# A recommendation tower on one TensorE: the second field comes by four gathers of whole rows and is turned by TensorE, and the first products run in another order

## The chip, the cores and the metric

One core of one Trainium2 chip runs the whole program. The metric is the device time of the program in microseconds (us), from start to end. Below, TensorE (PE in the profile), VectorE (DVE), ScalarE (ACT), GpSimd (POOL) and SyncE (SP) are the core's engines; GpSimd issues the gathers and the adding transfers here, SyncE the plain loads of weights.

## The reference

512 rows, 8 embedding tables of width 1024 (H). All is float32.

```
e = stack([tbl_f[ids[:, f]] for f in range(8)])          # 512 x 8 x 1024
t  = tanh(relu(e[:, not_idx] @ Wn1 + bn1) @ Wn2 + bn2)    # the two "not" fields; iv = e with these replaced
def pair_fuse(pairs, W1, b1, W2, b2):
    v = concat([iv[:, pairs[:, 0]], iv[:, pairs[:, 1]]])  # width 2048
    return relu(v @ W1 + b1) @ W2 + b2
z = (sum of 2 and-pairs + 1 or-pair + fields in no pair) / count
h = relu([z, dense_ctx] @ W_top1 + b_top1); h = relu(h @ W_top2 + b_top2); y = h @ W_top3
```

Which fields are "not" fields and which form pairs is an input (not_idx, and_pairs, or_pairs), so the rows to fetch are worked out on the chip.

## The kernel before, in words

**Layout.** Activations are held with the hidden index on the 128 partitions: XR has 8 buffers of 8 k-tiles x 512 batch columns. A float32 product is made of three fast ones: each operand is split into a rounded high part (ScalarE, an fp32r copy) and a low part (VectorE, the difference), and TensorE adds high x high, high x low and low x high. XO holds the split activations (8 k-tiles, so the operands of two entries), WO the split weights (two pieces), WR seven raw pieces of 512 KB as they come from memory.

**The work list.** The time line is a list of entries (a matrix product of a 512-wide quadrant, over 4 k-tiles) and each entry has 4 quarters t, one per PSUM bank of output. A quarter is 4 k x 3 = 12 matmuls of 128x512. The first 28 entries are three stages, in which two matrices of the batch's fields (Wn1 and then Wn2 for stages 0 and 1, Wa1 in two halves for stage 2) are multiplied by seven products instead of eight: P1, P2, Q5, Q6, Q7, P4, Q3. For it VectorE makes the sums S1, S3, S2, S4 of the activations' quadrants (operand_sum), and sums of weight quadrants are made by GpSimd's adding transfers (add_quadrant). Piece n serves quarters 2n and 2n+1. The quadrants of the activations of stage 0 are the halves of the two "not" fields: a11, a12 of the first and a21, a22 of the second, so P1 and P2 need only the first field, and S1 = a21 - a22 needs the second.

**What sets the order.** Each engine has a program written out by hand; at quarter t ScalarE and VectorE do, in this order, the split of weight piece t//2+1, the split of the next entry's operand, evacuations of PSUM (kept: ScalarE's copy; combine: VectorE's addition, then ScalarE's activation), the turning of gathered fields (TURNS_AT) and the sums (SUMS_AT). They are all in-order queues, tied by counting semaphores.

**Fields.** The first "not" field comes by four gathers of 128 whole rows (x0_in), is transposed by TensorE with the identity as weights (turn_x0), split by ScalarE and VectorE out of PSUM, and copied to XR (x0_raw). Every other field comes by 16 gathers of quarter rows (gather_half, 2 x 8; line 427) and is turned by four 32x32-block transposes of VectorE over 128x1024 (line 782). The first field that is so brought is slot 1, the second "not" field; slots 2 to 7 are the pairs. Ahead of them, VectorE computes the row numbers (slot_rows) and some constants; setup_done comes at the end of these.

**Start.** keep_running issues small products of the identity with itself, 28 of them while the first rows are on their way, so that TensorE isn't idle. The first product starts when all four tiles of the first field are turned (k-tiles 0 to 3). The third entry (Q5, the first that needs S1) runs in two halves of 256 columns each (BY_HALVES), so that its first half can start when half the batch of the second field is there.

Lines of the profile that matter: L950 all large products, L978 turns of the first field, L983 keep_running, L710 low part of weights, L521 high part, L765/L768/L771 low part of activations, L755 low part out of PSUM, L832 operand_sum, L846 combine, L915 the sum of weights for the first Q5, L782 the 32x32 turn, L421/L427 gathers, L440 adding transfers.

## Time and profile before

| | us |
|---|---|
| median of 3 runs | 548.82 (546.6 to 549.87) |
| the profiled execution, whole | 549.19 |
| its span, from the first to the last instruction | 547.1 |
| TensorE busy | 529.2 (97%) |
| VectorE busy | 360.5 (66%) |
| ScalarE busy | 242.4 (44%) |
| GpSimd busy | 242.5 (44%) |

The profiled execution is 0.4 us above the median, and 2.1 us of it lie around the span. Busy shares are averages over the span; what a stretch waits for is read from that stretch alone. A matmul's listed duration (about 390 ns) overlaps the next one's; the pace is read from a long row's time over its count.

### The profile page before, as it was taken

How to read it: one execution, taken by the hardware profiler on the slowest of the kernel's cores; microseconds unless marked ns; L12 is line 12 of the kernel's file. 1: busy time of each engine (PE TensorE's matmuls, PEld its weight loads, DVE VectorE, ACT ScalarE, POOL GpSimd, SP SyncE). 2: the span in 40 equal slices, each digit the busy share in tenths (PEclk: the TensorE clock that was granted, in tenths of full speed). 3: DMA queues.
4: the chain of work that ended last, by engine and by line, in shares of the span. 5: the costliest groups of instructions: out<-in, count | busy, mean ns of one | idle time of the engine just before them, and what ended most of it. 6: DMA issues, size and time to landing. Idle time of an engine off the chain costs nothing.

```text
span 547.1 us, 6141 instructions
## 1 busy us (share of the span) xinstructions
PE 529.2 (97%) x2392; PEld 438.8 (80%) x2392; DVE 360.5 (66%) x371; ACT 242.4 (44%) x291; POOL 242.5 (44%) x182
## 2 busy tenths in 40 slices
PE   6988999997999999999999999999999999999998
PEld 6868788885878888888888888888888888888885
DVE  7498886988757885888556678752332874245832
ACT  2733666626457544443536444323243423142343
POOL 5765877884888344130087017754445300000000
PEclk9999999998999999999999999999999999999999
DMA  7858965347786565367199425999999982331000
GB/s 260 298 168 162 196 205 177 108 127 119 156 205 195 118 115 177 78 100 131 38 195 314 127 98 167 276 246 247 248 247 246 246 264 80 115 93 40 1 0 1
DMA packets 38703, 87.31 MB, mean 160 GB/s; under 512 B 4401, under 2 KB 4657, under 8 KB 38674
## 3 DMA queue, kind: packets, MB, share of 16 engines
q0 software_dynamic: 18720, 49.29, 41.8%
q1 hardware_dynamic: 19522, 37.51, 21.5%
q8 instruction: 19, 0.31, 0.2%
q10 hardware_dynamic: 432, 0.11, 0.1%
q14 instruction: 10, 0.08, 0.0%
HBM read 86.90 MB, written 0.00 MB: 159 GB/s over the span
## 4 chain that ended last, share of the span: by engine, by line
PE 70%; POOL 14%; DVE 6%; DMA 4%; issue 4%; ACT 1%; DVEq 0%; ACTq 0%
PE PS L950 68%; POOL XR L427 12%; DMA WR<-weights 3%; DVE WO L710 2%; DVE XR L782 1%; DMA XR<-table,rows 1%; POOL XR L421 1%; POOL WR L440 1%; PE PS L1099 1%; DVE XR L832 1%; PE PS L1071 1%; DVE XR L846 1%; ACT WO L521 0%; DVE XO L765 0%; DMA XR<-ints 0%
## 5 line engine op out<-in xcount | busy, mean ns | idle before, releaser
L950 PE MATMUL PS<-XO,WO 128*128 128x512 f32 (+1 forms) x2256 | 506.3, 386 | 10.6 <-DVE WO L710 8.8
L950 PEld LDWEIGHTS PS<-XO,WO 128*128 128x128 f32 x2256 | 417.4, 188 | 97.5 <-DVE WO L710 10.9
L521 ACT ACTIVATE WO<-WR 128x1024 fp32r<-128x1024 f32 x93 | 98.6, 1060 | 254.6 <-PE PS L950 232.9
L710 DVE TENSOR_TENSOR WO<-WR,WO 128x1024 fp32r<-128x1024 f32 x93 | 113.7, 1224 | 144.4 <-ACT WO L521 144.2
L427 POOL DMA_INDIRECT XR<-table,rows x112 | 147.7, 1319 | 58.5 <-issue 33.5
L556 ACT ACTIVATE XO<-XR 128x1024 fp32r<-128x1024 f32 (+1 forms) x74 | 77.3, 1045 | 2.2 <-PE PS L950 1.9
L440 POOL DMA_DIRECT2D WR<-weights x30 | 37.2, 1627 | 85.7 <-DVE WO L710 59.6
L771 DVE TENSOR_TENSOR XO<-XR,XO 128x1024 fp32r<-128x1024 f32 x58 | 70.4, 1215 | 0.7 <-ACT XO L556 0.7
L498 POOL DMA_INDIRECT XR<-table,rows_rest x32 | 52.4, 1638 | 40.3 <-DMA XR<-table,rows_rest 38.5
L782 DVE STREAM_TRANSPOSE XR<-XR 128x1024 f32<-128x1024 f32 x28 | 59.7, 2137 | 4.3 <-DMA XR<-table,rows 4.3
L832 DVE TENSOR_TENSOR XR<-XR 128x1024 f32<-128x1024 f32 (+1 forms) x32 | 38.5, 1222 | 0.1
L561 ACT ACTIVATE XR<-XR,col 128x512 f32<-128x512 f32 x36 | 25.6, 715 | 11.0 <-DVE XR L846 11.0
L846 DVE TENSOR_TENSOR XR<-PS,XR 128x512 f32<-128x512 f32 x36 | 24.4, 679 | 3.5 <-PE PS L950 2.6
L587 ACT ACTIVATE XR<-PS 128x512 f32<-128x512 f32 x36 | 21.3, 594 | 6.2 <-PE PS L950 6.2
L768 DVE SCALAR_TENSOR_TENSOR XO<-XR,XO 128x1024 fp32r<-128x1024 f32 x16 | 19.5, 1218 | 0.3 <-ACT XO L556 0.2
L983 PE MATMUL PS<-ident 128*128 128x128 f32 x40 | 8.8, 392 | 5.0 <-DVE ident L700 5.0
L983 PEld LDWEIGHTS PS<-ident 128*128 128x128 f32 x40 | 8.2, 304 | 5.0 <-DVE ident L700 5.0
L860 DVE SCALAR_TENSOR_TENSOR XR<-PS,inv,XR 128x512 f32<-128x512 f32 x8 | 6.0, 750 | 6.5 <-PE PS L950 6.3
L592 ACT ACTIVATE XR<-PS,col 128x512 f32<-128x512 f32 x12 | 8.1, 677 | 0.7 <-PE PS L950 0.7
L755 DVE TENSOR_TENSOR XO<-PS,XO 128x512 fp32r<-128x512 f32 x8 | 5.0, 682 | 3.7 <-ACT XO L616 3.7
L616 ACT ACTIVATE XO<-PS 128x512 fp32r<-128x512 f32 x8 | 4.1, 603 | 7.2 <-PE PS L978 7.2
L865 DVE TENSOR_TENSOR XO<-XR,XO 128x512 fp32r<-128x512 f32 x4 | 2.8, 692 | 6.6 <-ACT XO L609 6.5
(68 smaller groups left out, 98.5 us busy)
## 6 DMA issues: line engine op xcount, KB each, us to landing
WR<-weights SPq DMA_DIRECT2D x71, 512.0 KB, 4.8
WR<-weights POOLq DMA_DIRECT2D x30, 512.0 KB, 8.1
XR<-table,rows POOLq DMA_INDIRECT x116, 3.9
XR<-table,rows_rest POOLq DMA_INDIRECT x32, 12.7
XR<-dense_t SPq DMA_DIRECT2D x3, 32.0 KB, 3.4
XR<-w_dense SPq DMA_DIRECT2D x3, 32.0 KB, 3.0
XR<-ints SPq DMA_DIRECT2D x1, 84.0 KB, 2.1
XR<-identity ACTq DMA_DIRECT2D x1, 64.0 KB, 3.6
```

The costliest lines, as they stand in the source:

```text
L427: pool.indirect_dma_start(to[:, QC * g:QC * (g + 1)], None, table_quarters, bass.IndirectOffsetOnAxis(ap=rows[:, slot - 1, 8 * h + g:8 * h ...
L440: pool.dma_start(raw_piece(slot), quadrant_rows(8 * matrix_of(e) + 4 * mh + 2 * h, kh), accum_op=ALU.add).then_inc(w_sum[slot], 16)
L498: pool.indirect_dma_start(rest_tile(b), None, table, bass.IndirectOffsetOnAxis(ap=rows_rest[:, b, f:f + 1], axis=0), compute_op=ALU.add if ...
L521: nc.scalar.activation(WO[:, n % 2, 0, :], WR[:, slot, :], ACT.Copy).then_inc(w_hi, 1)
L556: nc.scalar.activation(XO[:, s1:s1 + 2, 0, :], source(e, kk, regs), ACT.Copy, scale=scale)\
L561: nc.scalar.activation(place(s, which, m), place(s, which, m), FUNC[s], bias=bias_of(s, which, m)).then_inc(c_out[which], 1)
L710: V_.tensor_tensor(WO[:, n % 2, 1, :], WR[:, raw_slot(n), :], WO[:, n % 2, 0, :].bitcast(FP32), ALU.subtract).then_inc(w_lo, 1)
L771: V_.tensor_tensor(lo, source(e, kk, regs), hi, ALU.subtract).then_inc(x_lo, 1)
L782: V_.transpose(XR[:, SLOT_BUF[slot], :, b:b + 128].rearrange("p k (g b) -> p g k b", b=32), staging(slot, h)[:, 1024 * (i % 2):1024 * (i % ...
L832: V_.tensor_tensor(out, one, two, ALU.subtract).then_inc(sums, 1)
L846: V_.tensor_tensor(place(s, to, m), PS[:, BANK_B + m, :], place(s, to, m), op).then_inc(dve_ev, 1)
L950: mm = nc.tensor.matmul(PS[:, bank, cols], WO_t[:, slot, ws, i, k, :], XO[:, x0 + k, xs, cols], start=first and k == 0 and n == 0, stop=la ...
```

## The change

In words, in the order of the program:

- Row numbers of both "not" fields are computed together; the second field comes by four gathers of whole rows right behind the first's (x1_in), not by 16 of quarter rows. GpSimd then waits for setup_done before it gathers slots 2 and on.
- The first field is turned and split in two halves of the batch, in pairs of k-tiles: TensorE turns tiles 0 and 1 of the batch ahead of the first product, and tiles 2 and 3 between the products. Entry 0 (P1) is the one that runs in halves of 256 columns, and not Q5 any more.
- The second field is turned by 32 transposes of TensorE, 16 of them between the last products of entry 0 and 16 behind it; VectorE copies it from PSUM to XR by 8 copies (x1_keep). Its four 32x32 turns are gone.
- VectorE computes the pair slots' rows and the constants behind the low parts of the first half of the batch, and ahead of those of the second half.
- keep_running: 18 in place of 28, and 2+2+2 in place of 2+2+2+6.
- The products of stages 0 and 1 run in the order P1, P2, Q5, Q3, Q6, Q7, P4 (before: P1, P2, Q5, Q6, Q7, P4, Q3). Sums, loads, adding transfers, turns and evacuations move with it; P2 and Q5 (stage 0) and Q5 (stage 1) are now kept by ScalarE. Stages swap their halves of k and some buffers, so that each can start with what the one before has ready first.
- Stage 2 and what follows keep their order of products.

The diff, cut to its core:

```diff
-IDLE_PRODUCTS = 28
+ORDER = [(P1, P2, Q5, Q3, Q6, Q7, P4), (P1, P2, Q5, Q3, Q6, Q7, P4), (P1, P2, Q5, Q6, Q7, P4, Q3)]
+IDLE_PRODUCTS = 18
-BY_HALVES = 2
+KEPT = [{P1: "C11", P2: "C21", Q5: "C22", Q6: "C12"}, {P1: "C11", Q5: "C22", Q6: "C12"},
+        {P1: "C11", Q6: "C12", Q7: "C22"}]
+COMBINED = [{P2: ("C11", 9, 10), Q6: ("C12", 2, 3), Q7: ("C22", 1, 2)},
+            {P2: ("C11", 2, 3), Q6: ("C12", 2, 3), Q7: ("C22", 1, 2)}, ...
 SUMS_AT = {
-    (0, S1, 0): (2, 8), (0, S3, 0): (2, 9), (0, S2, 0): (9, 9), (0, S4, 0): (12, 13),
+    (0, S1, 0): (2, 3), (0, S3, 0): (4, 5), (0, S2, 0): (5, 6), (0, S4, 0): (7, 8),
-TURNS_AT = {1: (1, 1, 7, 7), 2: (15, 16, 19, 23), 3: (24, 27, 28, 32), 4: (36, 40, 44, 47),
+TURNS_AT = {2: (6, 8, 10, 12), 3: (14, 17, 19, 21), 4: (24, 27, 35, 38),
...
@@ SyncE
-            load(8)
+            load(6)
+            for n, split in ((7, 2), (10, 3), (11, 6), (16, 7)):
+                load_after(n, split)
@@ GpSimd
+            for b in range(BT):
+                pool.indirect_dma_start(flat(ROW1_BUF)[:, H * b:H * (b + 1)], None, table,
+                                        bass.IndirectOffsetOnAxis(ap=rows0[:, 1, b:b + 1], axis=0))\
+                    .then_inc(x1_in[b], 16)
-            pool.wait_ge(rows1_ready, 1)
+            pool.wait_ge(setup_done, 1)
             for h in range(2):
-                gather_half(1, h)
-            pool.wait_ge(setup_done, 1)
-            gather_half(2, 0, range(4))
-            for j in (Q6, Q7):
-                for h in range(2):
-                    add_piece(0, j, h)
-            gather_half(2, 0, range(4, 8))
+                gather_half(2, h)
+            gather_half(3, 0)
+            add_piece(0, Q7, 0)
+            for h in range(2):
+                add_piece(0, Q6, h)
+            add_piece(0, Q7, 1)
+            gather_half(3, 1)
...
@@ ScalarE
+            def x0_hi(h, pair):
+                act.wait_ge(x0_turned, x0_done(h, pair))
+                nc.scalar.activation(XO[:, 2 * pair:2 * pair + 2, 0, half_batch(h)], x0_bank(pair), ACT.Copy)\
+                    .then_inc(x_hi, 1)
+            def x0_keep(h, pair):
+                act.wait_ge(x_lo, x0_done(h, pair))
+                nc.scalar.activation(XR[:, 0, 2 * pair:2 * pair + 2, half_batch(h)], x0_bank(pair), ACT.Copy)\
+                    .then_inc(x0_raw, 1)
...
@@ VectorE
-            slot_rows(1, 1).then_inc(rows1_ready, 1)
-            slot_rows(2, 6)
             split_w(0)
             split_w(1)
+            for pair in range(4):
+                x0_lo(0, pair)
+            slot_rows(2, 6)
...
+            for pair in range(4):
+                x0_lo(1, pair)
+            def x1_keep(h):
+                for pair in range(4):
+                    dve.wait_ge(x1_turned, x0_done(h, pair))
+                    V_.tensor_copy(XR[:, 1, 2 * pair:2 * pair + 2, half_batch(h)], x0_bank(pair)).then_inc(x1_raw, 1)
+            x1_keep(0)
...
+                    if t == 2:
+                        x1_keep(1)
@@ TensorE
-            for b in range(BT):
+            for b in range(2):
                 pe.wait_ge(x0_in[b], 16)
                 for k in range(4):
...
+            def turn_second_field(h, first):
+                for k in range(first, first + 4):
+                    if k % 2 == 0:
+                        pe.wait_ge(*((x1_raw, x0_done(0, k // 2)) if h else (x0_raw, x0_done(1, k // 2))))
+                    for b in range(2 * h, 2 * h + 2):
+                        pe.wait_ge(x1_in[b], 16)
+                        turn = turn_rows(ROW1_BUF, b, k)
+                    if k % 2:
+                        turn.then_inc(x1_turned, 1)
...
+                            mm = product(bank0 + m, m // 2, m % 2, x0, i == 0, True,
+                                         x0_there if m == 0 else None, half_batch(i))
+                            if (i, m) == (0, 1):
+                                turn_second_half(0)
+                            elif (i, m) == (1, 0):
+                                turn_second_half(4)
+                            elif (i, m) == (1, 1):
+                                turn_second_field(0, 0)
+                            elif (i, m) == (1, 2):
+                                turn_second_field(0, 4)
+                    for k in (0, 4):
+                        turn_second_field(1, k)
```

The order of VectorE's instructions at its start. Each row is a line, an operation, out<-in by the program's names (XO split activations, WO split weights, PS PSUM) and a shape, with xN for N in a row. Before, the row numbers of the pair slots (L690, L694, L696) stand ahead of the first two weight splits:

```order
L706 TENSOR_SCALAR XR<-XR 128x8
L690 TENSOR_TENSOR XR<-XR 128x128 x6
L694 TENSOR_REDUCE XR<-XR 128x96
L696 CAST rows<-XR 128x96
L710 TENSOR_TENSOR WO<-WR,WO 128x1024 x2
L717 TENSOR_REDUCE XR<-XR 128x1
```

In the changed kernel the same place reads:

```order
L767 TENSOR_SCALAR XR<-XR 128x8
L771 TENSOR_TENSOR WO<-WR,WO 128x1024 x2
L777 TENSOR_TENSOR XO<-PS,XO 128x2x256 x4
L752 TENSOR_TENSOR XR<-XR 128x128 x6
L756 TENSOR_REDUCE XR<-XR 128x96
L758 CAST rows<-XR 128x96
L786 TENSOR_REDUCE XR<-XR 128x1
```

The row numbers, and all the constants behind them down to setup_done, now stand behind the low parts (L777) of the first half of the first field.

VectorE again, from the instruction that sets setup_done (L751, now L820) to the split of weight piece 4, the last rows here. Before:

```order
L751 TENSOR_SCALAR final_bias<-final_bias,inv 128x8
L755 TENSOR_TENSOR XO<-PS,XO 128x512 x8
L782 STREAM_TRANSPOSE XR<-XR 128x4x8x32 x2
L710 TENSOR_TENSOR WO<-WR,WO 128x1024
L832 TENSOR_TENSOR XR<-XR 128x4x256 x2
L915 TENSOR_TENSOR WR<-WR 128x1024 x2
L710 TENSOR_TENSOR WO<-WR,WO 128x1024
L846 TENSOR_TENSOR XR<-PS,XR 128x512 x2
L710 TENSOR_TENSOR WO<-WR,WO 128x1024
```

In the changed kernel (L830 is the copy of the second field, L906 operand_sum, L998 the sum of weights, L844 the low part of activations):

```order
L820 TENSOR_SCALAR final_bias<-final_bias,inv 128x8
L777 TENSOR_TENSOR XO<-PS,XO 128x2x256 x4
L830 COPY XR<-PS 128x2x256 x4
L771 TENSOR_TENSOR WO<-WR,WO 128x1024
L830 COPY XR<-PS 128x2x256 x4
L906 TENSOR_TENSOR XR<-XR 128x4x256
L998 TENSOR_TENSOR WR<-WR 128x1024 x2
L906 TENSOR_TENSOR XR<-XR 128x4x256
L771 TENSOR_TENSOR WO<-WR,WO 128x1024
L906 TENSOR_TENSOR XR<-XR 128x4x256
L844 TENSOR_TENSOR XO<-XR,XO 128x2x512
L906 TENSOR_TENSOR XR<-XR 128x4x256 x2
```

Piece 3's split (the second L771) is now behind eight copies, and behind it come four operations before piece 4's (L771, the next row, not shown), three of them sums.

GpSimd's queue from its first gathers on. Before (L427 are gathers of quarter rows, L440 adding transfers):

```order
L421 DMA XR<-table,rows 128x1024 x4
L427 DMA XR<-table,rows 128x256 x20
L440 DMA WR<-weights 128x2x512 x4
L427 DMA XR<-table,rows 128x256 x4
L440 DMA WR<-weights 128x2x512 x2
L427 DMA XR<-table,rows 128x256 x32
L440 DMA WR<-weights 128x2x512 x6
```

In the changed kernel (L480 and L494 are the same two kinds):

```order
L469 DMA XR<-table,rows 128x1024 x4
L473 DMA XR<-table,rows 128x1024 x4
L480 DMA XR<-table,rows 128x256 x24
L494 DMA WR<-weights 128x2x512 x4
L480 DMA XR<-table,rows 128x256 x8
L494 DMA WR<-weights 128x2x512 x2
L480 DMA XR<-table,rows 128x256 x8
L494 DMA WR<-weights 128x2x512 x2
```

The first adding transfers stand behind 24 gathers of quarter rows (20 before), and the run of 32 gathers ahead of stage 1's first additions is cut up into three runs of 8.

## Rows read from the trace of the kernel before

**Rows 1.** Busy time by stretch: stretch, its us, then each engine, TensorE's clock, DMA share, GB/s
```profile
16.00:60.00 44.00, 39.03 (x219) 33.43 (x220) 35.81 (x34) 22.22 (x33) 28.66 (x25) 1.00 0.78 215
...
165.00:537.00 372.00, 372.00 (x1658) 308.36 (x1657) 229.03 (x215) 156.18 (x177) 123.84 (x89) 1.00 0.62 154
```
**Rows 2.** Timeline of TensorE: start, us, what, xcount [idle before it <- who released it]
```profile
5.04 6.23 PE L983 MATMUL PS<-ident 128*128 128x128 f32 x28 [5.04 <-DVE ident L700]
...
16.14 2.99 PE L950 MATMUL PS<-XO,WO 128*128 128x512 f32 x12 [0.55 <-DVE XO L755]
18.97 1.93 PE L978 MATMUL PS<-ident,XR 128*128 128x128 f32 x16
20.66 8.44 PE L950 MATMUL PS<-XO,WO 128*128 128x512 f32 x36
31.32 5.76 PE L950 MATMUL PS<-XO,WO 128*128 128x512 f32 x24 [2.22 <-DVE WO L710]
37.22 8.65 PE L950 MATMUL PS<-XO,WO 128*128 128x512 f32 x48 [0.15 <-DVE WO L710]
47.08 3.13 PE L950 MATMUL PS<-XO,WO 128*128 128x256 f32 x24 [1.21 <-DVE WO L710]
50.63 6.01 PE L950 MATMUL PS<-XO,WO 128*128 128x256 f32 x48 [0.42 <-DVE XO L765]
57.47 65.59 PE L950 MATMUL PS<-XO,WO 128*128 128x512 f32 x288 [0.82 <-DVE XO L768]
127.02 34.27 PE L950 MATMUL PS<-XO,WO 128*128 128x512 f32 x144 [3.96 <-DVE WO L710]
162.52 326.86 PE L950 MATMUL PS<-XO,WO 128*128 128x512 f32 x1440 [1.23 <-DVE WO L710]
```
**Rows 3.** Busy time by stretch around the stall at 123 us (columns as in the first group)
```profile
127.00:130.00 3.00, 2.98 (x7) 2.40 (x8) 3.00 (x4) 2.04 (x4) 1.19 (x1) 0.51 0.28 20
```
**Rows 4.** Chain of waits, ahead of the stall at 123 us: start, us, what
```profile
107.33 9.56 POOL XR L427
117.19 0.94 POOL XR L427
118.13 6.50 DMA WR<-weights
```
**Rows 5.** The second gather's row in GpSimd's timeline, and line 421's landing
```profile
5.61 1.03 POOL L421 DMA_INDIRECT XR<-table,rows  x1 [0.30 <-issue]
...
DMA to landing us min/median/max: 4.6/5.3/5.4
```
**Rows 6.** Timeline of ScalarE and VectorE at the start and around 111 us
```profile
14.67 2.07 ACT L616 ACTIVATE XO<-PS 128x512 fp32r<-128x512 f32 x4 [6.31 <-PE PS L978]
15.30 2.48 DVE L755 TENSOR_TENSOR XO<-PS,XO 128x512 fp32r<-128x512 f32 x4 [1.27 <-ACT XO L616]
26.06 4.10 DVE L782 STREAM_TRANSPOSE XR<-XR 128x1024 f32<-128x1024 f32 x2 [3.33 <-DMA XR<-table,rows]
111.41 3.52 DVE L832 TENSOR_TENSOR XR<-XR 128x1024 f32<-128x1024 f32 x3
114.82 1.25 DVE L710 TENSOR_TENSOR WO<-WR,WO 128x1024 fp32r<-128x1024 f32 x1
```
**Rows 7.** Costliest groups, line 427: xcount | busy, mean ns | idle before, releaser
```profile
L427 POOL DMA_INDIRECT XR<-table,rows x112 | 147.7, 1319 | 58.5 <-issue 33.5
```
**Rows 8.** Line 440, adding transfers: ns min/median/max, then landing
```profile
L440 POOL DMA_DIRECT2D WR<-weights x30: 1179/1361/3180, 39.8 to 275.9; - x30
DMA to landing us min/median/max: 5.9/8.1/19.8
```
**Rows 9.** Timeline of VectorE's setup: its first and last rows
```profile
5.52 1.30 DVE L690 TENSOR_TENSOR XR<-XR 128x128 f32<-128x128 f32 x6
7.97 2.35 DVE L710 TENSOR_TENSOR WO<-WR,WO 128x1024 fp32r<-128x1024 f32 x2
13.81 0.23 DVE L751 TENSOR_SCALAR final_bias<-final_bias,inv 128x8 f32<-128x8 f32 x1
```

More of the change, by code:

```diff
@@ L128 @@
 R_SLOT = 4
-R_PIECES = [2 * e + h for s in range(3) for j in (P2, Q7, Q3) for half in range(STAGE_HALVES[s])
+R_PIECES = [2 * e + h for s in range(3) for j in ORDER[s] if j in (P2, Q7, Q3) for half in range(STAGE_HALVES[s])
             for e in [entry_of(s, j, half)] for h in range(2)]
@@ L271, in dlrm_tower @@
         quarter = sem("quarter")
[L272 removed]
+        field_in = {(s, h): sem(f"field_in{s}_{h}") for s in range(2, SLOTS) for h in range(2)}
         turned = sem("turned")
@@ L775, in turn @@
                 dve.wait_ge(field_in[slot, h], 16 * 8)
-                if i == 0 and slot > 1:
+                if i == 0 and slot == 2:
+                    dve.wait_ge(x1_turned, x0_done(1, 3))
+                if i == 0 and slot > 2:
                     dve.wait_ge(turned, turned_count(slot - 1, 1))
```

336 lines of the change are left out of this document (185 added, 151 removed), and 2 rows, old and new, of the table slot.

## The prediction

> **What bounds the kernel now.** I read the busy time by stretch first, then TensorE's timeline, then what each of its waits leads back to. From 165 us on TensorE is busy all of the time, while VectorE is busy for 229 of 372 us [rows 1]: nothing that the change moves there can bring time, as long as it hides. From 16 to 60 us TensorE is busy for 39.0 of 44 us and VectorE for 35.8. The timeline says where the rest is [rows 2]: the first product starts at 16.14; then TensorE idles 2.22, 0.15, 1.21, 0.42 and 0.82 us before it reaches quarter 12 at 57.47 (together 4.82), 3.96 before quarter 36 at 127.02, and 1.23 before quarter 48 at 162.52. That is 10.0 us of idleness behind the first product. The stall of 3.96 costs more than itself: behind it the granted clock stands at 0.50, the 1.2 GHz level, for three microseconds [rows 3]; the 144 matmuls from 127.02 took 34.27 us where the 1440 of the last row go at 0.227 us each, 32.7 for 144 [rows 2], so 1.5 us went with the clock. Its cause is GpSimd's queue: one gather held it for 9.56 us, and the adding transfer behind it landed 6.5 us after 118.13 [rows 4].
>
> **Prices.** From [rows 2]: a quarter of 12 full matmuls 2.72 us; one of 12 half-wide ones 6.01 / 4 = 1.50; a turn on TensorE (20.66 - 18.97) / 16 = 0.106, eight of them 0.85. From [rows 6]: a VectorE operation over 1024 columns starts (114.82 - 111.41) / 3 = 1.14 us behind the one before; a 32x32 turn 2.05; one over 512 columns out of PSUM 2.48 / 4 = 0.62; a ScalarE copy 2.07 / 4 = 0.52 over 512 columns, and so about 1.04 over 1024. The copy of the second field out of PSUM has no row; between half of 0.62 and a 1024-wide operation's 1.14 I take 0.62, since it reads as many columns from PSUM. The Trainium skill, VectorE: DVE Perf Modes, section The perf-mode tier table, holds an fp32 operation with a PSUM operand to one element a cycle for copies too, which speaks for 0.62 against its half; no row here shows such a copy.
>
> **The first product.** The second tile's gather starts at 5.61 and lands 5.3 us later [rows 5], and one more small multiplication stands before them (0.2): the second tile is there at about 11.1. Eighteen warm-up products at 6.23 / 28 = 0.22 us end at 9.0 [rows 2]. Then TensorE has 4 turns, 2 warm-ups, 8 turns and 2 warm-ups to do. At this time of before a small product still takes 0.22 us, a turn near 0.2: 3.1 us, so 14.2. The data are earlier: turned pair at 11.5, ScalarE at 11.7, VectorE 0.63 behind it [rows 6], product 0.84 behind that (16.14 - 15.30), 13.2. So TensorE itself decides: **14.2, 1.9 us earlier**.
>
> **Entry 0.** Four half quarters and 8 turns: to 21.1. The second half's low parts stand on VectorE behind the setup. VectorE has the first half's low parts done at about 16.1 (ScalarE must also copy two pairs to XR between them). The row numbers took 7.97 - 5.52 = 2.45 and the constants 14.04 - 10.32 = 3.7 us [rows 9]: setup_done at 22.3 (before 14.0), first low part of the second half lets the product run at 23.2. **Stall 2.1 us**. What is queued behind this: GpSimd, whose gathers of slot 2 wait for setup_done. Then 4 half quarters (6.0), 40 turns (4.2): entry 1 starts at 33.4. Their operands (copies of ScalarE, whole rows issued from 10.3 to 14.1 at the place of the first quarter-row gathers) are there some 3 us ahead, by a landing of 5.3; even the longest landing of an adding transfer, 19.8 [rows 8], behind 10.3 would cost only 3 us.
>
> **VectorE sets quarters 6 to 12.** It copies the second field's first half until 31.2 (the turns end at 30.3), then does piece 2's split, 4 copies, S1, two weight sums, S1, piece 3's split: 1.14 + 4 x 0.62 + 5 x 1.14 = 9.3, at 40.5. TensorE would be at quarter 6 at 33.4 + 5.45 = 38.9: **stall 1.7**. Then S3, x, S3, S2, piece 4: 5.7, at 46.2, TensorE ready at 46.0: **0.2**. Then x, a 32x32 turn, S2, S4, piece 5: 6.6, at 52.8, TensorE at 51.7: **1.1**. Then a turn and S4 (3.2), and here ScalarE is in the way: it can make the high part of Q3's operand only from S4, in front of piece 6's high part; 1.04 + 0.5 (a kept bank) + 1.04 + 1.14, so 59.9 or 60.0, TensorE ready at 58.3: **1.7**. Quarter 12 starts at 60.0; it was 57.47. So the start, whose field arrives by a shorter way, gives nothing back: **+2.5 us**. It is made of -1.9 (start), +3.4 (32 turns more) and 6.8 us of stalls for 4.8, which makes 3.5; the other -1.0 is what the rows of before run over my prices behind each wait (24 matmuls in 5.76 us for 5.45), and which isn't paid where VectorE sets the time.
>
> From quarter 12 to 24 VectorE has 12 splits, 6 turns and 10 combinations: 13.7 + 12.3 + 10 x 0.6 = 32.0 us, at 92.0, while TensorE comes to quarter 24 at 92.7. It hides by less than a microsecond, against the 2.7 us that each quarter lasts; if a combination costs 0.7, TensorE waits 0.3.
>
> **The two stalls of before.** Quarter 36 comes at 60.0 + 65.6 = 125.6 without a wait, if Q5's summed pieces of stage 1 are there. Their additions now stand behind runs of 8 gathers and not behind 32 in a row, and are issued as soon as VectorE has split P1's pieces, at about 102 and 107 us; they are needed at about 120, so that even a hold of 9.56 us would leave them in time. The 3.96 and its 1.5 of clock go. So does the 1.23 in front of P4: its additions stood behind eight gathers (the x8 and x2 of GpSimd's rows), and now follow the other additions at once, some seven quarters ahead of their use. From quarter 48 on the two kernels have the same work. Sum: +2.5 - 3.96 - 1.5 - 1.23 = **-4.2 us**. Against the profiled execution's 549.2 that is 545.0; the median of runs is 0.4 lower, so **544.6 us**. ScalarE's 4 kept banks more (2.1 us) hide under its 56% idle time.
>
> **Rivals.** (A) VectorE keeps up: the stalls of 1.7, 0.2, 1.1 and 1.7 vanish, because TensorE turns later or the copies cost half. 544.6 - 4.8 = **539.8**. For it: VectorE was idle for 8 of the 44 us of this stretch [rows 1], and 8.2 us of turns go for 5 of copies. Against it: its queue is in order, and the sums for the new order of products all come in quarters 2 to 8. (B) The first additions come late by a little: GpSimd issues 24 gathers behind 22.3, then adds. Piece 8's addition is issued at 22.3 + 24p + 1.5 and lands 8.1 later [rows 8]; ScalarE needs it at 70.9 (quarter 16) - 2.4 = 68.5. p was 1.32 + 0.3 of issue (33.5 / 112) on the mean, 1.62 with the long ones [rows 7], and 0.94 + 0.3 in a short one [rows 4], the bound from below: landing between 62.0 and 70.9. At 1.62 TensorE waits 2.4, **547.0**, which can't be told from no change. (C) The slower side: a hold of 9.56 us as in [rows 4] falls into these 24 gathers. From p = 1.4 (65.6) it adds 8.3: 5.4 us late, and as that is more than the 3.96 that brought the clock down, 1.5 on top: **551.5**. From such a delay on it is slower beyond what a measurement misses; at a p of 1.25 the same hold would end within it. Nothing in the rows says where such a hold falls; one of this length in 112 gathers [rows 4, 7] gives 24 of them a chance of about 0.2, and half of it hits where the margin is thin. (D) The clock falls in the stretch with the turns: at half rate the 96 half-wide matmuls cost 96 x 0.1 more and the 64 turns 6: up to 15 us, **559**. Against it: behind 16 turns in a row and behind a stall of 2.22 us the rows go at full pace [rows 2]. The Trainium skill, TensorE: Matmul & The Clock Gate, section Part 4: PE-mode transpose, says that transposes don't count as busy for the clock; by that rule this kernel, with runs of turns between short products, would be the place for (D), and it is the rule that speaks against the change.
>
> **The numbers.** Forecast as walked, between 542.5 (half of VectorE's stalls not there) and 546.5: 0.50. (A) 0.17. (B) 0.16. (C) 0.12. (D) 0.05. The range holds what lies between half-way past (A) and (B) with the lesser part of (C): 539.5 to 549.5, with 0.15 to 0.2 left out; the likeliest case's own is 542.5 to 546.5. A measurement of this kernel tells about 0.5% from no change, 2.7 us. Faster than 546.1: nearly all of the forecast's 0.50 and (A), 0.64. Same: (B) and a rest, 0.20. Slower than 551.5: half of (C) and more, (D): 0.16.
>
> **What would show it.** Right: first large product near 14.2; idle of about 2 us in front of entry 0's second half, released by VectorE's L777; waits of 1 to 2 us released by L771 at quarters 6, 10 and 12; quarter 12 near 60; no idle near 125 and 160, and a clock of 1.00 throughout. Wrong: a wait of ScalarE for an adding transfer near 68 us (B, C), a clock of 0.50 between 14 and 34 us (D), or quarter 12 before 57.5 (A).

## The result, and the profile after

The changed kernel is slower: 551.09 us (549.46 to 553.0, 20 runs) against 547.89 (540.82 to 551.5, 20 runs) for the kernel before, a ratio of 1.0089 [1.0066, 1.0112]. Ratios are taken over the runs within 1.5% of the fastest of their kernel, here 13 of the 20 of the kernel before; the means of all 20 give 1.0066. The profiled execution took 550.46, its span 548.7.

TensorE's timeline of the changed kernel, which answers to [rows 2]:
```profile
14.72 3.31 PE L1031 MATMUL PS<-XO,WO 128*128 128x256 f32 x24
...
23.29 1.70 PE L1031 MATMUL PS<-XO,WO 128*128 128x256 f32 x12 [1.48 <-DVE XO L777]
...
31.83 1.96 PE L1060 MATMUL PS<-ident,XR 128*128 128x128 f32 x16
33.55 5.71 PE L1031 MATMUL PS<-XO,WO 128*128 128x512 f32 x24
40.70 11.43 PE L1031 MATMUL PS<-XO,WO 128*128 128x512 f32 x48 [1.44 <-DVE WO L771]
53.01 5.76 PE L1031 MATMUL PS<-XO,WO 128*128 128x512 f32 x24 [0.88 <-DVE WO L771]
60.10 11.21 PE L1031 MATMUL PS<-XO,WO 128*128 128x512 f32 x48 [1.34 <-DVE WO L771]
75.50 415.39 PE L1031 MATMUL PS<-XO,WO 128*128 128x512 f32 x1824 [4.19 <-DVE WO L771]
```
Up to quarter 12 it runs as walked: there at 60.10. The stalls of 3.96 and 1.23 us of [rows 2] are gone, and 1824 matmuls follow one another from quarter 16 on. But in front of quarter 16 stands a stall of 4.19 us that the kernel before doesn't have. The chain of waits names it (start, us, what):
```profile
22.91 0.95 POOL XR L480
...
61.18 0.94 POOL XR L480
62.12 0.79 POOL WR L494
62.91 10.20 DMA WR<-weights
73.14 1.06 ACT WO L575
74.23 1.24 DVE WO L771
75.50 4.54 PE PS L1031 x12
```
The lines left out are 22 more gathers and the 0.30 us of issue ahead of each. GpSimd issues 24 gathers in a row, (62.12 - 22.91) / 24 = 1.63 us each, then the first adding transfer, which lands 10.2 us later; ScalarE and VectorE pass its piece on, and TensorE, free since 71.31, had nothing to multiply. The granted clock was 1.00 before the stall and 0.50, the 1.2 GHz level, behind it. Busy time by stretch (PE, PEld, DVE, ACT, POOL, granted clock, DMA share, GB/s):
```profile
16.00:60.00 44.00, 38.96 (x233) 33.55 (x232) 38.41 (x69) 19.26 (x29) 30.38 (x23) 1.00 0.52 172
77.00:80.00 3.00, 3.00 (x9) 2.33 (x8) 3.00 (x4) 1.88 (x3) 2.69 (x3) 0.50 1.10 261
```
At the pace of [rows 2], 0.227 us, the 1824 matmuls take 414.0; they took 415.4, so the clock cost 1.4 us. The new stall costs 5.6 us with its clock. The two old ones cost 3.96 + 1.23 + 1.5 = 6.7, so the tail gains 1.1; quarter 12 comes 60.10 - 57.47 = 2.6 later. Together that is the 1.6 by which the spans differ (548.7 against 547.1).

What stretches the gathers stands in the timelines of GpSimd and VectorE side by side:
```profile
33.70 0.95 POOL L480 DMA_INDIRECT XR<-table,rows  x1 [0.30 <-issue]
34.95 1.97 POOL L480 DMA_INDIRECT XR<-table,rows  x1 [0.30 <-issue]
...
46.31 1.97 POOL L480 DMA_INDIRECT XR<-table,rows  x1 [0.30 <-issue]
48.59 0.95 POOL L480 DMA_INDIRECT XR<-table,rows  x1 [0.30 <-issue]
...
32.49 2.48 DVE L830 COPY XR<-PS 128x512 f32<-128x512 f32 x4
34.89 1.21 DVE L906 TENSOR_TENSOR XR<-XR 128x1024 f32<-128x1024 f32 x1
...
46.24 1.22 DVE L844 TENSOR_TENSOR XO<-XR,XO 128x1024 fp32r<-128x1024 f32 x1
47.38 2.20 DVE L857 STREAM_TRANSPOSE XR<-XR 128x1024 f32<-128x1024 f32 x1
```
While VectorE copies from PSUM or turns 32x32 blocks a gather takes 0.95 us, as at 33.70 and 48.59. From 34.89 to 47.38 VectorE does operations with two operands in SBUF one behind the other, and all six gathers of that time take 1.96 or 1.97: each ends 0.9 us behind the next start of an operation (the gather of 34.95 at 36.92, the operation's start at 36.02). In all, the 24 gathers take 39.2 - 24 x 1.25 = 9.2 us more than short ones would.

The 9.56 us of [rows 4] look like the long form of it. VectorE's timeline of the kernel before:
```profile
106.91 1.21 DVE L771 TENSOR_TENSOR XO<-XR,XO 128x1024 fp32r<-128x1024 f32 x1
108.02 1.24 DVE L832 TENSOR_TENSOR XR<-XR 128x1024 f32<-128x1024 f32 x1
...
115.96 2.17 DVE L782 STREAM_TRANSPOSE XR<-XR 128x1024 f32<-128x1024 f32 x1
```
Between these stand six more operations with two SBUF operands, the last at 114.82 [rows 6]. The gather starts at 107.33, inside the first of the eight, is held over the seven boundaries between them, and ends at 116.89, 0.93 behind the start of the 32x32 turn. The Trainium skill, SBUF — State Buffer, section SBUF: two separate sides, describes the port pair that VectorE and GpSimd share as an exclusive lock, held for the whole instruction; a VectorE operation with two SBUF inputs takes it only against a GpSimd operation that reads SBUF, and where the page has GpSimd unable to write descriptors it speaks of another kind, an operation of VectorE in a 2-port mode. The traces agree with a lock by a two-input operation, as far as a gather, whose row numbers lie in SBUF, is held to the end of one (1.97); a hold over seven boundaries between operations the page doesn't have.

### The profile page after: what moved, and what is told of

The parts are those of the page before. It is cut to its first block, busy times and chain, and to the rows that moved or that the text cites. A ratio compares the mean times of both kernels' runs of the same rounds, so it can differ in the third digit from the quotient of the medians.

```text
span 548.7 us, 6197 instructions
## 1 busy us (share of the span) xinstructions
PE 531.1 (97%) x2408; PEld 440.8 (80%) x2408; DVE 357.4 (65%) x373; ACT 244.4 (45%) x295; POOL 218.3 (40%) x170
## 4 chain that ended last, share of the span: by engine, by line
PE 86%; POOL 6%; DMA 3%; DVE 2%; issue 2%; ACT 1%
PE PS L1031 84%; POOL XR L480 6%; DMA WR<-weights 2%; DMA XR<-table,rows 1%; PE PS L1211 1%; PE PS L1183 1%; DMA XR<-ints 0%; DVE XO L777 0%; PE PS L1218 0%; DVE WO L771 0%; DVE XR L752 0%; ACT XR L665 0%; POOL XR L469 0%; ACT XO L659 0%; ACT WO L575 0%
## 5 line engine op out<-in xcount | busy, mean ns | idle before, releaser
L771 DVE TENSOR_TENSOR WO<-WR,WO 128x1024 fp32r<-128x1024 f32 x93 | 113.9, 1225 | 148.3 <-ACT WO L575 148.0
L480 POOL DMA_INDIRECT XR<-table,rows x96 | 119.7, 1246 | 67.5 <-issue 28.0
L604 ACT ACTIVATE XO<-XR 128x1024 fp32r<-128x1024 f32 (+1 forms) x76 | 79.4, 1046 | 16.1 <-DVE XR L906 14.2
L494 POOL DMA_DIRECT2D WR<-weights x30 | 37.2, 1598 | 101.8 <-DVE WO L771 68.8
L844 DVE TENSOR_TENSOR XO<-XR,XO 128x1024 fp32r<-128x1024 f32 x60 | 73.2, 1221 | 2.7 <-ACT XO L604 2.7
L857 DVE STREAM_TRANSPOSE XR<-XR 128x1024 f32<-128x1024 f32 x24 | 51.6, 2151 | 0.0
L906 DVE TENSOR_TENSOR XR<-XR 128x1024 f32<-128x1024 f32 (+1 forms) x32 | 38.4, 1217 | 0.0
L929 DVE TENSOR_TENSOR XR<-XR,PS 128x512 f32<-128x512 f32 x16 | 11.1, 691 | 2.2 <-PE PS L1031 2.1
L1060 PE MATMUL PS<-ident,XR 128*128 128x128 f32 x64 | 10.4, 314 | 1.3 <-DMA XR<-table,rows 1.3
L929 DVE TENSOR_TENSOR XR<-PS,XR 128x512 f32<-128x512 f32 x16 | 10.8, 679 | 1.3 <-PE PS L1031 1.3
L1065 PE MATMUL PS<-ident 128*128 128x128 f32 x24 | 6.1, 423 | 4.6 <-DVE ident L761 4.6
L1060 PEld LDWEIGHTS PS<-ident,XR 128*128 128x128 f32 x64 | 8.8, 199 | 1.7 <-DMA XR<-table,rows 1.7
L777 DVE TENSOR_TENSOR XO<-PS,XO 128x512 fp32r<-128x512 f32 x8 | 5.1, 685 | 6.3 <-ACT XO L659 6.3
L1065 PEld LDWEIGHTS PS<-ident 128*128 128x128 f32 x24 | 5.6, 332 | 4.6 <-DVE ident L761 4.6
```

Source lines behind the costliest of these rows:

```text
L480: pool.indirect_dma_start(to[:, QC * g:QC * (g + 1)], None, table_quarters, bass.IndirectOffsetOnAxis(ap=rows[:, slot - 2, 8 * h + g:8 * h ...
L494: pool.dma_start(raw_piece(slot), quadrant_rows(8 * matrix_of(e) + 4 * mh + 2 * h, kh), accum_op=ALU.add).then_inc(w_sum[slot], 16)
L604: nc.scalar.activation(XO[:, s1:s1 + 2, 0, :], source(e, kk, regs), ACT.Copy, scale=scale)\
L771: V_.tensor_tensor(WO[:, n % 2, 1, :], WR[:, raw_slot(n), :], WO[:, n % 2, 0, :].bitcast(FP32), ALU.subtract).then_inc(w_lo, 1)
L844: V_.tensor_tensor(lo, source(e, kk, regs), hi, ALU.subtract).then_inc(x_lo, 1)
L857: V_.transpose(XR[:, SLOT_BUF[slot], :, b:b + 128].rearrange("p k (g b) -> p g k b", b=32), staging(slot, h)[:, 1024 * (i % 2):1024 * (i % ...
```

## The experiments

Each ratio is against the kernel before on the same chip, beside the kernel named. The kernel before takes about 548 us on some chips and 565 on others; every kernel profiled on the latter, w1 nearly excepted, shows gaps of TensorE before quarter 12 which no instruction releases, so totals of the two kinds of chip aren't compared. The tail, from quarter 12's first product to the end of the span, can be: it is 489.6 before and 488.6 after. "c1 = a1" means the same kernel again. The profiled executions (the stalls of 2.94 in a1, 0.75 in w1, 2.17 in w2, 2.22 in g1 and 0.58 in i2 lie behind 290 us and are gaps that nothing releases, not waits for GpSimd; they are in the tail's time):

| kernel | quarter 12 at | tail | longest stall in the tail | median (before beside it) | ratio |
|---|---|---|---|---|---|
| a1 additions first | 76.02 | 491.5 | 2.94, 2.70 | 569.07 (565.96) | 1.0089 [1.0037, 1.0141] |
| b later gathers apart | 73.36 | 484.9 | 1.36 | 566.14 (565.96) | 1.0014 [0.9968, 1.0059] |
| c0 the changed kernel | 59.27 | 489.8 | 4.58 | 550.86 (547.64) | 1.0089 [1.0049, 1.0129] |
| c1 = a1 | 59.47 | 489.5 | 2.97 | 550.81 | 1.0068 [1.0031, 1.0105] |
| c2 setup earlier | 58.05 | 488.9 | 2.85 | 550.14 | 1.0064 [1.0018, 1.011] |
| c3 both | 60.94 | 488.2 | 2.94 | 551.20 | 1.0089 [1.0039, 1.0139] |
| w1 changed, few gathers | 62.15 | 483.6 | 0.75 | 547.32 (565.18) | 0.9653 [0.959, 0.9716] |
| w2 before, few gathers | 68.98 | 484.9 | 2.17 | 554.92 | 0.9812 [0.9724, 0.99] |
| d1 a1 + late turns | 74.94 | 484.3 | 0.47 | 561.42 | 0.995 [0.9919, 0.998] |
| g1 changed + memsets | 86.21 | 485.0 | 2.22 | 572.38 | 1.0108 [1.0031, 1.0186] |
| i1 before + memsets | 73.44 | 483.0 | none | 559.75 (564.52) | 0.997 [0.992, 1.0019] |
| i2 = g1 | 84.32 | 483.3 | 0.58 | 571.83 | 1.0171 [1.011, 1.0231] |
| i3 = d1 | 74.68 | 484.3 | 0.56 | 561.10 | 0.9977 [0.9941, 1.0013] |
| i4 = d1 + memsets | 75.26 | 483.0 | none | 560.39 | 0.9967 [0.9932, 1.0002] |
| j1 = i4 | 59.44 | 483.9 | 0.62 | 545.87 (548.35) | 0.9964 [0.9936, 0.9991] |
| j2 = i1 | 57.55 | 482.5 | none | 541.83 | 0.9888 [0.9847, 0.9929] |

**The additions ahead of slot 3's gathers (a1, c1).** The theory at first: the first additions are late behind 24 gathers, and nothing else is wrong.
```
+            add_piece(0, Q7, 0)
+            for h in range(2):
+                add_piece(0, Q6, h)
             gather_half(3, 0)
-            add_piece(0, Q7, 0)
-            for h in range(2):
-                add_piece(0, Q6, h)
             add_piece(0, Q7, 1)
```


> The changed kernel, with GpSimd's three adding transfers for Q7 and Q6 moved ahead of slot 3's first eight gathers; nothing else. Theory (late additions): the changed kernel loses 4.19 us of idleness in front of quarter 16 and about 1.4 us of clock behind it because those transfers are issued only at 62.1 us, behind 24 gathers that took 39.2 us. Then this kernel issues the first two near 49 us and the third near 53, the stall at 71.3 us and the 0.50 clock behind it are gone, quarter 12 stays at 60.1, and the time falls by 5.6 us, from 551.1 to about 545.5. Rival (the additions are slow by themselves, by contention with the loads and each other, 10.2 us to landing): they still land late, the stall shrinks by less than half, and the time stays above 549.

> Again the changed kernel with three adding transfers ahead of slot 3's first eight gathers. Theory (late additions): no stall in front of quarter 16, and 5.6 us below the changed kernel of the same chip. Rival (contention makes them late wherever they stand): less than 2.5 us below it.

c1's TensorE timeline behind quarter 12:
```profile
59.47 16.63 PE L1031 MATMUL PS<-XO,WO 128*128 128x512 f32 x72 [1.32 <-DVE WO L771]
76.49 27.89 PE L1031 MATMUL PS<-XO,WO 128*128 128x512 f32 x120 [0.39 <-DVE WO L771]
107.35 383.86 PE L1031 MATMUL PS<-XO,WO 128*128 128x512 f32 x1680 [2.97 <-DVE WO L771]
```
The stall at quarter 16 is gone, 0.39 stands at quarter 18 (76.49) and 2.97 at quarter 28 (107.35), with 1680 matmuls that take 2.5 us over pace behind it. The theory expected 5.6 us less and got 0.05 (550.81 against c0's 550.86): it fell. VectorE's timeline shows the new place:
```profile
95.39 1.21 DVE L771 TENSOR_TENSOR WO<-WR,WO 128x1024 fp32r<-128x1024 f32 x1
100.92 2.19 DVE L857 STREAM_TRANSPOSE XR<-XR 128x1024 f32<-128x1024 f32 x1 [4.32 <-DMA XR<-table,rows]
104.94 1.23 DVE L844 TENSOR_TENSOR XO<-XR,XO 128x1024 fp32r<-128x1024 f32 x1 [1.83 <-issue]
```
VectorE waits 4.32 us for slot 4's gathers at its turn in quarter 24, then idles another 1.83 for nothing that the profile names, and the split that TensorE needs is queued behind. What GpSimd puts first it takes from what it puts last.

**Setup in VectorE's early gap, and both (a2, c2, a3, c3).** slot_rows moves ahead of split_w(0), the first half's low parts behind the constants, so that GpSimd starts earlier. c0 is the changed kernel unedited beside them.
```
+            slot_rows(2, 6)
             split_w(0)
             split_w(1)
-            for pair in range(4):
-                x0_lo(0, pair)
-            slot_rows(2, 6)
...
+            for pair in range(4):
+                x0_lo(0, pair)
             for pair in range(4):
                 x0_lo(1, pair)
```


> The changed kernel, with VectorE's row numbers ahead of its first two weight splits and the constants right behind these, in front of the first half's low parts; GpSimd's queue is untouched. VectorE idled 2.3 us ahead of the first split and 2.9 us behind the second in the changed kernel, and the moved work is 6.1 us. Theory: setup_done comes near 14 and not at 22.6 us, the stall of 1.48 us in front of entry 0's second half goes, gathers of quarter rows start near 15 and not at 22.9, so the additions are issued near 54 and the 4.19 us in front of quarter 16 go too, with their clock: about 544. The first product may move by up to 1 us (14.7 to 15.5). Rival (the early DMA traffic is the limit: gathers that start 8 us earlier collide with the weight loads and only stretch): additions issued after 58 us and a time above 548.

> Both moves together. Theory: no stall in front of quarter 16 and none in front of entry 0's second half; the additions have a margin of ten microseconds or more. As VectorE alone then sets quarters 6 to 12, the time is that of the setup move within 0.5 us, about 544. Rival (they add up beyond it): below 542.

> The changed kernel itself, unedited, beside the next two on one chip. The runs so far of the kernels with a moved piece were on a chip where the kernel before takes 566 us and TensorE idles between single instructions with nothing that the profile names (gaps of 0.3 to 2.4 us between 20 and 45 us). Expectation: if this chip is like the first one, 551 us, a stall of about 4.2 us in front of quarter 16 and a clock of 0.50 behind it; if such gaps appear again, 1.009 times before or more.

> Again the changed kernel with VectorE's setup in its idle gaps. Theory (setup_done comes too late): the stall ahead of entry 0's second half and that ahead of quarter 16 gone, 7 us below the changed kernel of the same chip. Rival, formed on the other chip: gathers that start at 15 us keep the DMA engines full from 18 to 40 us, and TensorE's gaps between single instructions come with it, so that entry 0 takes 10 to 30 us longer and the kernel is slower than the changed one. A gain says the gaps belong to that chip, a loss that they belong to the traffic.

> Again both moves. Theory: as the setup move within 0.5 us. Rival (gaps from traffic): slower than the kernel with the additions moved alone, by what its gaps between 18 and 45 us show.

a2 and a3 took 1.0199 [1.0125, 1.0272] and 1.011 [1.0068, 1.0153]; a2's profiled execution, at 589.05 far above its median of 576.43, isn't read. The theory of a gain of 7 us fell on both kinds of chip. c2 has the stall of entry 0 gone and quarter 12 at 58.05, 1.2 ahead of c0, and loses it again: 1.99 at 87.53 and 2.85 at 135.20. GpSimd's timeline, then VectorE's, shows where the last comes from:
```profile
110.97 7.06 POOL L480 DMA_INDIRECT XR<-table,rows  x1 [0.30 <-issue]
118.33 1.02 POOL L480 DMA_INDIRECT XR<-table,rows  x1 [0.30 <-issue]
...
114.73 2.35 DVE L906 TENSOR_TENSOR XR<-XR 128x1024 f32<-128x1024 f32 x2
117.22 1.23 DVE L771 TENSOR_TENSOR WO<-WR,WO 128x1024 fp32r<-128x1024 f32 x1
```
The one gather lasts from 110.97 to 118.03; VectorE's only gap in that time, 114.73 + 2.35 = 117.08 to 117.22, stands 0.95 ahead of its end. Four orders of the same work on one chip, four tails of 488 to 490: where the stall falls depends on the order; that there is one holds in all four.

**The kernel before, with Q5's additions of stage 1 ahead of slot 4's gathers (b).**
```
+            for h in range(2):
+                add_piece(1, Q5, h)
             gather_half(4, 0)
-            for j in (Q5, Q6, Q7):
+            for j in (Q6, Q7):
                 for h in range(2):
                     add_piece(1, j, h)
-            gather_half(4, 1)
             for h in range(2):
                 add_piece(1, P4, h)
+            gather_half(4, 1)
```


> The kernel before, with GpSimd's run of gathers ahead of stage 1's additions cut: the two additions for Q5 go ahead of slot 4's first eight gathers, and the last eight behind P4's additions. Theory (the stall of 3.96 us before quarter 36 and the 1.23 before quarter 48 hang on GpSimd's queue, and how long the gathers take differs from execution to execution, which is why the 20 runs of before spread over 540.8 to 551.5 while the changed kernel's lie within 549.5 to 553.0): no stall behind quarter 12, a spread under 4 us and a median of about 542. Rival (the spread comes from elsewhere, such as the start): median within 1 us of before, spread as wide.

The tail of its profiled execution is short, with one stall of 1.36, but its runs spread from 560 to 580 and the median, 0.2 above the kernel before, tells nothing. By the signs named in advance it was the rival that came out; with the early gaps of this chip in every run, the pair doesn't decide.

**Few gathers (w1, w2).** Slots 2 to 4 of the changed kernel and of the kernel before fetch their bytes by 2 gathers of whole rows per half for 8 of quarter rows. The rows are those of another field, so the output isn't the reference's; every other operation is unchanged, but for the count that VectorE's turns wait for.
```
+                if slot in (2, 3, 4):
+                    for g in range(2 * min(groups) // 8, 2 * (max(groups) + 1) // 8):
+                        pool.indirect_dma_start(
+                            to[:, H * g:H * (g + 1)], None, table,
+                            bass.IndirectOffsetOnAxis(ap=rows0[:, 0, 2 * h + g:2 * h + g + 1], axis=0),
+                        ).then_inc(field_in[slot, h], 16)
+                    return
...
-                dve.wait_ge(field_in[slot, h], 16 * 8)
+                dve.wait_ge(field_in[slot, h], 16 * (2 if slot in (2, 3, 4) else 8))
```


> The changed kernel with slots 2, 3 and 4 fetched by 2 gathers of whole rows per half in place of 8 of quarter rows: the same bytes, 12 gathers for 48. The rows are those of another field and lie otherwise, so the values are wrong; every later operation is unchanged. Theory (GpSimd's queue is the bound of both kernels from quarter 12 to 36, and only the place of the stall moves): no stall behind quarter 12, span about 543.5 and time about 545.3, as the walk along VectorE's queue gave. Rival (the bytes or the additions' landing are the bound): the stall in front of quarter 16 stays above 2 us and the time above 548.

> The same edit in the kernel before (slots 2 to 4, 12 gathers for 48, values wrong in the same way). Theory: the stalls of 3.96 and 1.23 us at quarters 36 and 48 go, with their clock; the start's stalls stay, so quarter 12 stays at 57.5 and the time is about 542.5. The changed kernel's direct cost, quarter 12 later by 2.6 us, then stands alone between this kernel and the one above: 2 to 3 us. Rival: the new order costs more than that (a difference above 4 us) or nothing (below 1).

w1's TensorE timeline from quarter 12:
```profile
62.15 234.21 PE L1038 MATMUL PS<-XO,WO 128*128 128x512 f32 x1032 [1.32 <-DVE WO L778]
297.11 190.85 PE L1038 MATMUL PS<-XO,WO 128*128 128x512 f32 x840 [0.75 <-issue]
```
1032 matmuls at 0.227 and no stall; w2 has the same (1032 in 234.23). Without the gap behind 290 us both tails are 482.8. So the tails of 488 to 490 are GpSimd's doing: 6.8 us in the kernel before and 5.8 in the changed one, near the 6.7 and 5.6 worked out above. Whether by the count of gathers or by what holds them, this pair doesn't tell: w2 still has a gather of 5.03 us, at 142.43, which costs TensorE nothing. The times, expected at 545.3 and 542.5, are 547.32 and 554.92: w2 has the early gaps of its chip, w1 next to none, so that their difference isn't the price of the start.

**Slot 4's turns later (d1, i3).** On top of a1: `4: (24, 27, 35, 38)` becomes `4: (36, 40, 44, 47)`, the quarters of the kernel before.

> The changed kernel with the additions moved ahead of slot 3's gathers, and with slot 4's four 32x32 turns at quarters 36, 40, 44 and 47, as before, in place of 24, 27, 35 and 38. With the additions moved alone VectorE stood 4.3 us at slot 4's first turn, waiting for its gathers, with the split of piece 13 queued behind it, and TensorE lost 2.97 us there. Theory: that stall goes too, with what follows it: 545.5, 5 us below the changed kernel. Rival (a third place takes its turn): above 548.5.

> The changed kernel with three additions ahead of slot 3's gathers and slot 4's turns at quarters 36 to 47 (d1 again). With both waits for GpSimd's gathers given time, the tail from quarter 12 is 484 and the total about 2.6 above a kernel that starts as before does: 545 to 547, ratio 0.996 to 1.000. Rival: another wait of GpSimd's queue takes their place, and the ratio is 1.005 to 1.009 as for c0 to c3.

Both tails are 484.3, with 0.47 and 0.56 the longest stalls: where what waits for it comes later, the queue has the time that it takes. In each a gather of 3.8 us at 83 did no harm. i3's ratio is the expected one; d1's total can't be held against its 545.5, as the chip is of the slower kind.

**Gaps in VectorE's runs (g1, i1, i2, i4, j1, j2).** The memset tests what holds a gather. One of one column, 0.06 us, stands ahead of each split and each sum that VectorE makes up to quarter 55, 67 operations with two SBUF operands; its operations on finished products (combine) have none. g1, i1, i2 and j2 change nothing on GpSimd; i4 and j1 have the memsets on top of d1.
```
+            def breathe():
+                ticks[0] += 1
+                V_.memset(tick[:, ticks[0] - 1:ticks[0]], 0.0)
...
             def split_x(e, kk):
...
+                if e < 14:
+                    breathe()
...
+                if s < 2:
+                    breathe()
                 V_.tensor_tensor(out, one, two, ALU.subtract).then_inc(sums, 1)
...
+                        if t < 56:
+                            breathe()
                         split_w(t // 2 + 1)
```


> The changed kernel with a one-column memset on VectorE ahead of each of its 67 two-operand operations (splits and sums) of stages 0 and 1. In all traces so far a long hold of a gather ends 0.95 us behind the moment at which VectorE turns to a one-operand operation or idles. Theory: with a short one-operand operation in between, no gather is held beyond one VectorE operation (2.1 us), and the mean stays near 1.25 or falls. Rival (the holds hang on something else): holds above 2.5 us or a mean above 1.4. The time is no test: the memsets cost VectorE some 4 us in its full stretch.

> The kernel before, with a one-column memset on VectorE ahead of each of its two-operand operations up to quarter 55, so that no two of them stand back to back. If the holds of GpSimd's gathers last as long as such operations follow each other without a gap, no gather before 170 us takes above some 3 us (before: 9.56, 5.05 and 3.69), both stalls of TensorE in that stretch go, and the kernel gains nearly all of their 4.2 us: ratio 0.993 to 0.997 (some 544 where the kernel before takes 548), less 0.4 for the memsets. Rival: the holds are the DMA engines' or the count of gathers; then they stay, at the same places, and the ratio is 1.000 to 1.003.

> The changed kernel with the same one-column memsets (g1 again, beside kernels of the same chip). If the holds cost it the stall at quarter 16 and no more, that stall is gone and the tail from quarter 12 is 484 to 485 where the changed kernel had 488.6: 545 to 547, ratio 0.996 to 1.000. Rival: the traffic of the gathers in the early stretch is what costs, whatever VectorE does; then the stall is there and the ratio is near 1.008.

> Both edits of the two kernels beside it. If both only free TensorE from GpSimd's queue, nothing adds up: the tail is 484 again and the time within 1.5 of each of them. If each frees only a part of it, this one is the fastest of the three by over 2 us.

> i4 again, on another chip. If nothing but GpSimd's queue made the changed kernel slower, quarter 12 starts at 59 to 60.5 on a chip without the early gaps of TensorE and the tail from there is 483.0 to 484: a span of 543 to 544, some 545 in all, ratio 0.994 to 0.998. On a chip with those gaps: 560, ratio 0.990 to 0.997. If the memsets and the late turns only shift the stall, the ratio is 1.004 or more.

> i1 again, beside j1: the kernel before with the same cure. Its quarter 12 starts 1.8 to 2.6 earlier than j1's and its tail is 483.0 to 484 as well: ratio 0.990 to 0.994 (some 543 where the kernel before takes 548), so that the second field's turning by TensorE is worth a loss of 2 us once the queue is out of the way. If the change had a gain of its own apart from the stalls, j1 would be no slower than j2.

j2 decides between hold and count: it issues as many gathers as the kernel before, and at the place of [rows 4] GpSimd's and VectorE's timelines read
```profile
106.19 0.95 POOL L428 DMA_INDIRECT XR<-table,rows  x1 [0.30 <-issue]
107.45 1.67 POOL L428 DMA_INDIRECT XR<-table,rows  x1 [0.30 <-issue]
109.42 1.99 POOL L428 DMA_INDIRECT XR<-table,rows  x1 [0.30 <-issue]
111.41 2.62 POOL L441 DMA_DIRECT2D WR<-weights  x2
...
108.19 1.25 DVE L843 TENSOR_TENSOR XR<-XR 128x1024 f32<-128x1024 f32 x1
108.24 0.06 DVE L713 MEMSET tick<- 128x1 f32 x1
109.34 1.24 DVE L717 TENSOR_TENSOR WO<-WR,WO 128x1024 fp32r<-128x1024 f32 x1
```
Here the gather at 107.45 takes 1.67 where the one at 107.33 took 9.56, and the additions go out at 111.41, not at 118.13. VectorE's operations start 1.15 us apart (109.34 - 108.19), for 1.13 before ((114.82 - 106.91) / 7), so that a memset costs some 0.02. TensorE's timeline of j2:
```profile
57.55 424.64 PE L963 MATMUL PS<-XO,WO 128*128 128x512 f32 x1872 [0.84 <-DVE XO L777]
```
and of j1:
```profile
59.44 16.61 PE L1044 MATMUL PS<-XO,WO 128*128 128x512 f32 x72 [1.35 <-DVE WO L778]
76.67 16.66 PE L1044 MATMUL PS<-XO,WO 128*128 128x512 f32 x72 [0.62 <-DVE WO L778]
93.52 392.00 PE L1044 MATMUL PS<-XO,WO 128*128 128x512 f32 x1728 [0.19 <-DVE WO L778]
```
j2 has all 1872 products from quarter 12 to the turns of the end without a stall. Its six runs lie between 540.68 and 542.46, where those of the kernel before spread from 543.57 to 551.76 beside it. That fits holds that differ from run to run, but isn't shown: one execution of the kernel before was traced, and j1, with memsets, spreads over 4.4 us, no less than c1 without them (3.8). The fastest runs of the kernel before on other chips (540.82, and 541.27 beside c0) are as fast as j2's. In 14 profiled executions without the memsets, 11 have a gather before 200 us that holds the queue for over 3 us (not after, c0 and w1); in the six with them there is none. c1 and j1 differ by the memsets and the late turns, and at the same place have 3.84 (at 67.53) and 1.55 (at 67.52).

By its own words g1 met the rival: it expected no hold beyond 2.1 us and named 2.5 as the sign against it, and one took 2.66 (2.63 in i2). g1's timelines of GpSimd and VectorE:
```profile
93.20 2.66 POOL L481 DMA_INDIRECT XR<-table,rows  x1 [0.30 <-issue]
...
94.30 0.68 DVE L940 TENSOR_TENSOR XR<-XR 128x512 f32<-128x512 f32 x1
94.91 1.22 DVE L778 TENSOR_TENSOR WO<-WR,WO 128x1024 fp32r<-128x1024 f32 x1
```
The hold passes 94.30, where combine has no memset, and ends at 95.86, 0.95 behind 94.91, where the split has one. So here GpSimd got in at the first boundary with a memset. It doesn't undo the wait for that boundary: six gathers of j1 between 34 and 48 us take 1.97 to 1.99, as they do after.

i4 is within 0.7 us of i3, as expected if both edits free TensorE from the same queue, and j1's ratio is in its range. j2 came out below its range (0.9888 for 0.990 to 0.994), 4.0 us ahead of j1 where 2 were expected. i1 gained 4.8 us by the medians, but its interval takes in no change, since the early gaps of those chips scatter both kernels. i2 missed its time: no stall for GpSimd is in the tail of g1 or i2, but quarter 12 comes at 86.21 and 84.32, which gives the additions 24 us more, so that its absence proves nothing. i4, with a1's order, has it at 75.26 on the chip of i2. GpSimd's last gather of the first row starts in i4 at 41.26, in i2, which has eight more in the row, at
```profile
51.45 0.95 POOL L481 DMA_INDIRECT XR<-table,rows  x1 [0.30 <-issue]
```
and VectorE's copies out of PSUM go on at 45.14 in i4 and, but for one in between, at
```profile
52.86 0.69 DVE L837 COPY XR<-PS 128x512 f32<-128x512 f32 x1 [6.99 <-issue]
```
in i2. On those chips the compute engines nearly stand still as long as a row of quarter-row gathers lasts: from 35 to 45 us of i4 TensorE is busy for 1.0 of 10 us, VectorE for 0.0 and ScalarE for 0.6. Eight more gathers at 1.25 us are 10 us, and i2's quarter 12 is 9.1 later. Memsets alone on the changed kernel, on a chip without this, weren't timed, so that j1's 5 us against c1 aren't split between memsets and late turns. The stall of 4.19 itself they would hardly have removed, since gathers of 1.97 us keep their length beside them; in j1 it is gone with a1's order.

## Why the prediction was wrong

**The first product, entry 0, quarters 6 to 12: right.** 14.72 for 14.2 (the second tile came 1.10 after TensorE was ready); the second half of entry 0 at 23.29 for 23.2, with a stall of 1.48 for 2.1; then 1.44, 0.88 and 1.34 for 1.7, 1.1 and 1.7, all released by L771, and quarter 12 at 60.10 for 60.0 (the terms written down for the last wait add up to 59.7). The copy out of PSUM, which had no row, costs (34.89 - 32.49) / 4 = 0.60 for the 0.62 taken. The later quarter 12, forecast at 2.5 us, is 60.10 - 57.47 = 2.6 in the two profiles and 59.44 - 57.55 = 1.9 between j1 and j2.

**(A) and (D): neither.** VectorE did set the time. The granted clock is 1.00 from 16 to 60, with 48 of the 64 turns among and behind the half-wide products (16 stand ahead of them), where the Trainium skill, TensorE: Matmul & The Clock Gate, section Part 4: PE-mode transpose, was held against the change; this trace gives no sign of it. The 0.50 read here stands behind the stall of 4.19.

**The stalls of before go: right.** None is left at 125 or 160. But of the 6.7 us that they cost, 5.6 are paid again at quarter 16.

**The step that failed: "The two stalls of before" ends the sum where it should have gone on along GpSimd's queue.** The 24 gathers and piece 8's addition stood in the prediction as rival (B), with 0.16, though its own mean pitch of 1.62 gave a stall of 2.4 us; only a pitch below (68.5 - 8.1 - 1.5 - 22.3) / 24 = 1.53 gave none. The pitch was 1.63. The rest of (B) was sized too small: start of the gathers 0.6 later, landing 10.2 for 8.1, issue 0.7 less, and 0.3 by the pitch, 2.3 us in all, so 73.11 for 70.8; and the clock's 1.4 was counted for (C) alone. With these terms the prediction's own sum is -4.2 + 4.19 + 1.4 = +1.4 on the profiled 549.2, or 550.6; the profile has 550.46. That 551.09 lies beside (C)'s 551.5 is luck: no hold of (C)'s kind was in these 24 gathers, whose longest took 1.97.

**The second: one execution taken for the kernel.** The stall at 123 us was credited in full, 5.5 us with its clock. But the kernel before spreads over 10.7 us, and its median of 20 is 1.3 us below the profiled execution, for the 0.4 that the prediction used; the changed kernel's is 0.6 above its own. The loss of 3.2 us by the medians is these two and the 1.3 by which the profiled executions differ. That the spread comes from holds of different length is likely but not shown.

**What the forecast's number means.** 544.6 was the changed kernel without any wait for GpSimd. j1 comes nearest to it: 545.87, its profiled execution 545.09. But the kernel before, with the memsets alone, is at 541.83. The change gives nothing by itself: 4.0 us slower by the medians, of which 1.9 is the start and 0.8 two stalls in the tail; no row accounts for the other 1.3. In the forecast it gained because its order of products moves stage 1's additions out of a run of gathers.

## What to carry to other kernels

Where a queue of descriptors made by GpSimd feeds the critical path, it can pay to keep VectorE from doing operations with two SBUF operands back to back: a one-column memset between them cost 0.02 us each and made the kernel before 1.1% faster (j2, 0.9888 [0.9847, 0.9929]); on a chip with the early gaps no change was clear (i1, 0.997 [0.992, 1.0019]). When work is reordered, follow each in-order queue with its mean pitch to the first transfer that is needed, and take that as the forecast and not as a rival. A stall seen in one execution of a kernel whose runs spread by 2% is not the stall of its median.
